# Two heads side by side in the 64-row halves of the matmul array, for the scores and their maxima in a fused attention kernel

## The chip, the cores and the metric

The kernel runs on one core of one Trainium2 chip. The metric is the device time of one launch in microseconds; the lower the better. Times given for a kernel are medians of several executions; what is read from a trace comes from one more, profiled, execution.

## What is computed

The input is 32 images of 128 channels by 32 x 32 positions, so 1024 tokens of 128 channels each. Every image goes through three layers:

```python
# layer 0: group norm, one-head attention over 1024 tokens (width 128), residual
h = group_norm(x)
q, k, v = split(qkv_w @ h + qkv_b)
x = x + proj(softmax(q.T @ k / sqrt(128)) @ v)
t = tokens(x)
# layer 1: eight search heads of width 16, two shared retrieval values
u = layer_norm(t)
sq, sk, rq = heads(u @ wq_s), heads(u @ wk_s), heads(u @ wq_r)      # 8 heads of 16
rv = u @ wv_r                                                        # 2 values of 16
retrieved = softmax(sq @ sk.T / 4) @ rv                              # per head and value
gate = softmax(sum(rq * (retrieved @ wk_ret)) / 4)                   # over the 2 values
t = t + (sum(gate * retrieved)) @ w_out
# layer 2: a block-quantised 128 x 128 weight and a second weight
t = t + (layer_norm(t) @ lora.T) @ W.T
```

The eight heads' score matrices of 1024 x 1024 are the bulk: each is made twice, once for the row maxima and once, transposed and with the maximum subtracted, for the exponentials.

## The kernel before

An image's layer 1 is worked in four **phases** (two groups of four heads by two halves of 512 queries) of eight **steps** (key tiles of 128), 32 steps in all. A software pipeline runs over the images: in one pass of the loop the scores and values of image b (`HEAD`), the last stages of image b-1 (`TAIL`) and the first ones of b+1 and b+2 (`FRONT`, `NEXT`) stand mixed. `schedule()` makes the list: for each step, which stages are issued and in which order, from a position between 0 and 1 that each gets. Every engine runs the same list in program order (`in_order`), takes what is its own, and waits on semaphores for the rest. Images 1 to 29 are a hardware loop (`engine.Fori`, L213), the first and last three are written out.

The stages that matter here:

- `scores` (L799 on TensorE, PE for short): one matmul for one head, key tile by 512 queries, into one PSUM bank; ScalarE (ACT) reads it with an exponential into `p1` (L982). Four a step.
- `max1` (L776): the same product the other way round (query tile by 512 keys) for the *next* phase; VectorE (DVE) takes the row maximum (L1072). 32 a phase, spread over the steps so that VectorE's load is even.
- `max_rows1` (L784): at the end of a phase the maxima, negated by VectorE (L1076), are transposed by TensorE, and ScalarE writes the rows into `q_stack` (L950). The next phase's scores wait for it.
- `values` (L810): rv times `p1` for four heads at once, four matmuls of 32 output columns side by side, two passes each (fp32). GpSimd (POOL) adds the same `p1` into `p_sum` (L627), seven adds a phase, and `den` (L819) sums that over the partitions once a phase, two steps into the next one. GpSimd's first add of a phase waits until `den` of the phase before has been read (L990).
- All of these share six PSUM banks (`ps_bank`), taken in turn. A matmul waits until the reader of its bank, six uses back, is done.

The operands are kept as a high and a low part. For a head, `q_stack` and `k_stack` hold three blocks of 32 rows (hi/hi, hi/lo, lo/hi) of which the head uses 16 in each block, and a fourth block of 32 rows for the maxima; `max1` reads 96 rows, `scores` 128. SyncE (SP) builds these stacks from SBUF to SBUF with 36 DMAs an image (L541, L546).

## Time and profile before

| | |
|---|---|
| median of 3 runs | 5834.74 us (5830.56 to 5835.21) |
| the profiled execution | 5838.83 us, its span 5836.5 us |
| TensorE matmul | 5436.7 us busy, 93% |
| GpSimd | 4251.2 us, 73% |
| VectorE | 3955.0 us, 68% |
| ScalarE | 3470.2 us, 59% |
| granted TensorE clock | 0.981 of full |

Busy time of TensorE counts a matmul from its start to its modelled end. Matmuls are pipelined, so the next may start before that; what one costs is the distance from its start to the start of the next, which the timeline shows.

### The profile page before, as it was taken

What the parts mean: (1) busy time and instruction counts of PE and PEld (TensorE: products, weight loads), DVE (VectorE), ACT (ScalarE), POOL (GpSimd) and SP (SyncE); (2) the same over time, 40 slices, a digit from 0 to 9 for tenths busy, and PEclk for the clock granted to TensorE, in tenths of its full rate; (3) what the DMA queues carried; (4) which work ended last, traced back from release to release, by engine and by line L of the source; (5) the groups of instructions that cost most, each with busy time, mean ns of one, the idle gap of its engine ahead of it and who ended that gap; (6) DMA issues with size and microseconds to landing.
All of it is one profiled execution on the core that took longest, in us unless ns stands there. A gap on an engine that the chain in (4) does not pass through costs nothing.

```text
span 5836.5 us, 99943 instructions
## 1 busy us (share of the span) xinstructions
PE 5436.7 (93%) x30350; PEld 3295.9 (56%) x30350; DVE 3955.0 (68%) x8189; ACT 3470.2 (59%) x6689; POOL 4251.2 (73%) x1109
## 2 busy tenths in 40 slices
PE   5999999999999999999999999999999999999986
PEld 3555555565555555555555555555555555556543
DVE  4776667667676666676667676677766676766763
ACT  2566566656566565666565665666665656665654
POOL 1677777777777777777777777777777777777787
PEclk9999999999999999999999999999999999999998
DMA  1101110111111111111111111111111111101110
GB/s 36 24 26 33 31 38 26 27 34 27 38 26 34 27 34 30 37 26 30 31 27 38 31 29 27 34 30 38 26 34 27 27 37 36 28 24 36 23 33 11
DMA packets 64867, 176.65 MB, mean 30 GB/s; under 512 B 21856, under 2 KB 23264, under 8 KB 64224
## 3 DMA queue, kind: packets, MB, share of 16 engines
q1 hardware_dynamic: 64224, 168.61, 12.3%
q8 instruction: 339, 5.55, 0.4%
q14 instruction: 304, 2.49, 0.1%
HBM read 17.53 MB, written 16.78 MB: 6 GB/s over the span
## 4 chain that ended last, share of the span: by engine, by line
PE 79%; DVE 9%; ACT 5%; issue 4%; POOL 2%; SPq 0%; DMA 0%; DVEq 0%; ACTq 0%; POOLq 0%
PE ps_bank L776 16%; PE ps_u L810 16%; PE ps_bank L799 15%; PE ps_bank L763 7%; PE ps_bank L691 4%; PE ps_bank L679 3%; DVE max_part L1062 3%; DVE max_part L1072 3%; PE ps_bank L747 2%; PE ps_bank L819 2%; PE ps_bank L750 2%; PE ps_bank L749 2%; PE ps_bank L748 2%; POOL p_sum L627 2%; ACT work L963 2%
## 5 line engine op out<-in xcount | busy, mean ns | idle before, releaser
L627 POOL TENSOR_TENSOR p_sum<-p_sum,p 128x2048 f32<-128x2048 f32 x768 | 3509.0, 4569 | 411.4 <-ACT p L982 381.2
L1072 DVE TENSOR_REDUCE max_part<-ps_bank 128x1 f32<-128x512 f32 x4096 | 2613.7, 683 | 1237.9 <-PE ps_bank L776 1224.9
L982 ACT ACTIVATE p<-ps_bank 128x512 f32<-128x512 f32 x4096 | 2283.6, 599 | 1495.3 <-PE ps_bank L799 1482.6
L799 PE MATMUL ps_bank<-q_stack,k_stack 128*128 128x512 f32 x4096 | 1726.3, 438 | 25.1 <-DVE t_front L1096 20.7
L776 PE MATMUL ps_bank<-k_stack,q_stack 96*128 96x512 f32 x4096 | 1594.6, 426 | 25.9 <-DVE max_part L1072 11.2
L776 PEld LDWEIGHTS ps_bank<-k_stack,q_stack 96*128 96x128 f32 x4096 | 777.6, 193 | 687.5 <-DVE max_part L1072 287.2
L627 POOL TENSOR_TENSOR p_sum<-p 128x2048 f32<-128x2048 f32 x128 | 584.3, 4565 | 792.4 <-ACT den_sb L990 731.3
L799 PEld LDWEIGHTS ps_bank<-q_stack,k_stack 128*128 128x128 f32 x4096 | 766.2, 192 | 655.1 <-issue 273.2
L810 PE MATMUL ps_u<-p,rv 128*32 128x512 f32 x8192 | 1114.5, 617 | 19.1 <-ACT u_sb L987 12.2
L763 PEld LDWEIGHTS ps_bank<-v,p 128*128 128x128 f32 x4096 | 494.1, 191 | 17.8 <-issue 2.4
L763 PE MATMUL ps_bank<-v,p 128*128 128x129 f32 x4096 | 498.2, 274 | 1.6 <-ACT p L939 1.6
L939 ACT ACTIVATE p<-ps_bank 128x512 f32<-128x512 f32 x512 | 306.3, 598 | 325.1 <-PE ps_bank L750 322.1
L1062 DVE TENSOR_REDUCE max_part<-ps_bank 128x1 f32<-128x512 f32 x512 | 316.9, 681 | 117.8 <-PE ps_bank L728 117.8
L810 PEld LDWEIGHTS ps_u<-p,rv 128*32 128x32 f32 x8192 | 162.5, 108 | 369.1 <-issue 298.2
L747 PE MATMUL ps_bank<-q_hi,k_hi 128*128 128x512 f32 x512 | 219.2, 428 | 112.4 <-issue 87.7
L605 POOL TENSOR_TENSOR rstd<-var,minus_half 128x8 f32<-128x8 f32 x64 | 105.6, 1650 | 273.7 <-DVE var L1109 273.7
L749 PE MATMUL ps_bank<-max_row,first_row 128*128 128x512 f32 x512 | 204.6, 400 | 0.0
L750 PE MATMUL ps_bank<-q_hi,k_lo 128*128 128x512 f32 x512 | 204.2, 399 | 0.0
L748 PE MATMUL ps_bank<-q_lo,k_hi 128*128 128x512 f32 x512 | 203.9, 398 | 0.0
L747 PEld LDWEIGHTS ps_bank<-q_hi,k_hi 128*128 128x128 f32 x512 | 97.7, 191 | 181.5 <-issue 152.1
L1095 DVE RECIPROCAL den<-ps_bank 128x1 f32<-128x1 f32 x256 | 41.9, 164 | 213.6 <-PE ps_bank L763 211.8
L728 PE MATMUL ps_bank<-k_hi,q_hi 128*128 128x512 f32 x512 | 167.3, 418 | 2.3 <-DVE k_lo L1054 1.6
(140 smaller groups left out, 4600.2 us busy)
## 6 DMA issues: line engine op xcount, KB each, us to landing
q_stack<-q_hi SPq DMA_DIRECT2D x256, 128.0 KB, 2.4
k_stack<-k_hi SPq DMA_DIRECT2D x512, 64.0 KB, 2.3
x_sb<-in_x SPq DMA_DIRECT2D x32, 512.0 KB, 3.3
t_held<-t_front SPq DMA_DIRECT2D x32, 512.0 KB, 2.9
k_stack<-k_lo SPq DMA_DIRECT2D x256, 64.0 KB, 2.4
q_stack<-q_lo SPq DMA_DIRECT2D x128, 128.0 KB, 2.3
t_core<-t_held SPq DMA_DIRECT2D x32, 512.0 KB, 3.4
out_y<-out_sb SPq DMA_DIRECT2D x32, 512.0 KB, 2.6
```

What stands on the lines that cost most here:

```text
L627: pool.tensor_tensor(p_sum[:, :, :], before, p1[:, step % ring, :, :], ALU.add)\
L747: pe.matmul(out, k_hi[0][:, keys], q_hi[0][:, queries], start=True, stop=False)
L748: pe.matmul(out, k_hi[0][:, keys], q_lo[0][:, queries], start=False, stop=False)
L749: pe.matmul(out, first_row[:, :], max_row0[:, queries], start=False, stop=False)
L750: pe.matmul(out, k_lo[0][:, keys], q_hi[0][:, queries], start=False, stop=True).then_inc(filled, 1)
L763: last = pe.matmul(out[:, 0:P + 1], p0[:, key_tile, at:at + P], v0[:, key_tile, :], start=(key_tile == 0), stop=(key_tile == tiles - 1))
L776: pe.matmul(out, q_stack[0:3 * QUAD, head // 2, at:at + P], k_stack[0:3 * QUAD, head, half * HALF:(half + 1) * HALF], start=True, stop=Tru ...
L799: pe.matmul(out, k_stack[:, head, keys], q_stack[:, head // 2, queries], start=True, stop=True)\
L810: last = pe.matmul(ps_u[n * QUAD:(n + 1) * QUAD, :], rv[:, key_tile, :], p1[:, step % ring, n, :], start=(key_tile == 0), stop=(key_tile = ...
L982: act.activation(p1[:, step % ring, n, :], read_bank(), ACT.Exp, scale=scale1)\
L1062: dve.tensor_reduce(max_part0[:, i, half:half + 1], read_bank(), AXIS.X, ALU.max)\
L1072: dve.tensor_reduce(max_part1[:, i, n, half:half + 1], read_bank(), AXIS.X, ALU.max)\
```

## The change

Five edits, made together.

1. The three products of a head are laid out with interleaved rows (`PARTS` = 4: rows 0, 4, 8, ... hold the first, 1, 5, 9, ... the second), so that a head needs 64 rows instead of 128. The heads of a pair lie in rows 0 to 63 and 64 to 127 of both stacks. `max1` and `scores` then take 63 and 64 rows, and each pair of matmuls stands next to each other in the list.
2. The stacks are built with 24 DMAs an image of 32 rows each. Rows 63 and 127 hold the maxima: ScalarE writes them to `max_row1`, and SyncE moves them with two DMAs a phase (`move_rows`); the next phase's scores wait for these.
3. No maxima stand in the last step of a phase: 32 uses are dealt, in twos, to the first seven steps. `max_rows1` stands at 0.05 of the last step instead of 0.85. All maxima stand right behind pairs of scores.
4. `values` of two steps are issued together in every second step, and `den` stands beside them. The transposes of the maxima turn 128 columns instead of 32.
5. The loops get `hint_back_edge=True`.

```diff
 for phase in range(4):
-        load[7] += LAST_STEP_LOAD
-        for _ in range(32):
-            least = min(range(8), key=lambda n: load[n] + count[n])
-            count[least] += 1
+        for _ in range(16):
+            least = min(range(7), key=lambda n: load[n] + count[n])
+            count[least] += 2
...
-            behind = ("HEAD", "values", step - 1) if step else ("TAIL", "values", 31)
-            placed.append((VALUES_AT if n else 0.02, behind))
-            placed += [(SCORES_AT + SCORES_SPREAD * m, ("HEAD", "scores", (step, m))) for m in range(4)]
-            end = 0.75 if n == 7 else 1.0
-            placed += [(end * (m + 0.5) / len(maxima), one) for m, one in enumerate(maxima)]
+            if step % 2 == 0:
+                for late in (2, 1):
+                    behind = ("HEAD", "values", step - late) if step else ("TAIL", "values", 32 - late)
+                    placed.append((VALUES_AT if n else 0.02, behind))
+            placed += [(VALUES_AT, one) for one in steps[step] if one[1] == "den"]
+            placed += [(SCORES_AT + SCORES_SPREAD * 2 * (m // 2), ("HEAD", "scores", (step, m))) for m in range(4)]
+            placed += [(SCORES_AT + SCORES_SPREAD * 2 * (m // 2), one) for m, one in enumerate(maxima)]
             if n == 7:
-                placed.append((0.85, (image, "max_rows1", ahead)))
+                placed.append((0.05, (image, "max_rows1", ahead)))
...
-    with engine.Fori(1, images - 2) as b:
+    with nc.Fori(1, images - 2, engines=[engine.engine], hint_back_edge=True) as b:
...
-                            sp.dma_start(q_stack[part * QUAD:(part + 1) * QUAD, pair, :].bitcast(F32),
-                                         q_part[1][pair * QUAD:(pair + 1) * QUAD, :].bitcast(F32))\
-                              .then_inc(stacked[group], 16)
-                            for n in range(2):
-                                at, row = pair * QUAD + n * HEAD_DIM, part * QUAD + n * HEAD_DIM
-                                sp.dma_start(k_stack[row:row + HEAD_DIM, 2 * pair + n, :].bitcast(F32),
-                                             k_part[1][at:at + HEAD_DIM, :].bitcast(F32))\
-                                  .then_inc(stacked[group], 16)
+                            sp.dma_start(q_stack[part:2 * ROWS:PARTS, pair, :].bitcast(F32),
+                                         q_part[1][source, :].bitcast(F32)).then_inc(stacked[group], 16)
+                            sp.dma_start(k_stack[part:2 * ROWS:PARTS, pair, :].bitcast(F32),
+                                         k_part[1][source, :].bitcast(F32)).then_inc(stacked[group], 16)
+                def move_rows(b, phase):
+                    group, half = divmod(phase, halves)
+                    sp.wait_ge(max_row_ready[1], phases * b + phase + 1)
+                    for pair in range(GROUP // 2):
+                        sp.dma_start(q_stack[ROWS - 1:2 * ROWS:ROWS, group * GROUP // 2 + pair,
+                                             half * HALF:(half + 1) * HALF].bitcast(F32),
+                                     max_row1[2 * pair:2 * pair + 2, :].bitcast(F32)).then_inc(rows_moved, 16)
...
-                    pe.matmul(out, q_stack[0:3 * QUAD, head // 2, at:at + P],
-                              k_stack[0:3 * QUAD, head, half * HALF:(half + 1) * HALF],
+                    rows = slice(side * ROWS, (side + 1) * ROWS - 1)
+                    pe.matmul(out, q_stack[rows, pair, at:at + P],
+                              k_stack[rows, pair, half * HALF:(half + 1) * HALF],
                               start=True, stop=True).then_inc(filled, 1)
...
-                        pe.wait_ge(max_row_ready[1], phases * b + phase + 1)
-                        awaited = (max_row_ready[1],)
+                        pe.wait_ge(rows_moved, row_incs * (phases * b + phase + 1))
-                    pe.matmul(out, k_stack[:, head, keys], q_stack[:, head // 2, queries], start=True, stop=True)\
+                    pair, side = divmod(GROUP * group + n, 2)
+                    rows = slice(side * ROWS, (side + 1) * ROWS)
+                    pe.matmul(out, k_stack[rows, pair, keys], q_stack[rows, pair, queries], start=True, stop=True)\
                       .then_inc(filled, 1)
```

How this moves instructions, on TensorE first. The place is the seventh step of the first phase, in the loop body. `ps_bank<-q_stack,k_stack` is a score, `ps_bank<-k_stack,q_stack` a maximum, `ps_u<-p,rv` the values of four heads. Before:

```order
L645 ISA
L799 MATMUL ps_bank<-q_stack,k_stack 128x512
L645 REGISTER_ALU
L776 MATMUL ps_bank<-k_stack,q_stack 128x512
L645 REGISTER_ALU
L799 MATMUL ps_bank<-q_stack,k_stack 128x512
L808 ISA
L810 MATMUL ps_u<-p,rv 32x512 x4
L645 REGISTER_ALU
L799 MATMUL ps_bank<-q_stack,k_stack 128x512
```

After:

```order
L677 ISA
L831 MATMUL ps_bank<-q_stack,k_stack 128x512
L677 REGISTER_ALU
L831 MATMUL ps_bank<-q_stack,k_stack 128x512
L677 REGISTER_ALU
L809 MATMUL ps_bank<-k_stack,q_stack 128x512
L677 REGISTER_ALU
L809 MATMUL ps_bank<-k_stack,q_stack 128x512
L842 MATMUL ps_u<-p,rv 32x512 x4
L840 ISA
L842 MATMUL ps_u<-p,rv 32x512 x4
L831 MATMUL ps_bank<-q_stack,k_stack 128x512 x2
```

Scores and maxima stood singly and in turn; now they come in twos of one kind, and two steps' values follow each other.

The second place is the last step of that phase on TensorE, where the maxima are turned. Before, they come behind the step's scores:

```order
L810 MATMUL ps_u<-p,rv 32x512 x4
L645 REGISTER_ALU
L799 MATMUL ps_bank<-q_stack,k_stack 128x512
L645 REGISTER_ALU
L799 MATMUL ps_bank<-q_stack,k_stack 128x512
L781 REGISTER_ALU
L645 REGISTER_ALU
L784 MATMUL ps_bank<-ident,max_cols 32x128 x4
```

After, they stand ahead of all four scores:

```order
L795 MATMUL ps_bank<-v,p 128x129 x8
L814 REGISTER_ALU
L677 REGISTER_ALU
L817 MATMUL ps_bank<-ident,max_cols 128x128 x4
L677 REGISTER_ALU
L831 MATMUL ps_bank<-q_stack,k_stack 128x512
```

The turning moved ahead of four scores that had stood before it.

The third is SyncE's queue in the loop, from the stack of one group to the next image's. After:

```order
L561 DMA q_stack<-max_row 2x512 x2
L567 DMA out_y<-out_sb 128x1024
L578 DMA t_core<-t_held 128x1024
L561 DMA q_stack<-max_row 2x512 x2
L573 DMA t_held<-t_front 128x1024
L551 DMA q_stack<-q_hi 32x1024
```

Before, the three big transfers stood there alone; the moves of the maxima are new between them.

## Rows read from the trace of the kernel before

**Rows 1.** The page: span, busy time by engine, and the chain that ended last

```profile
span 5836.5 us, 99943 instructions
PE 5436.7 (93%) x30350; PEld 3295.9 (56%) x30350; DVE 3955.0 (68%) x8189; ACT 3470.2 (59%) x6689; POOL 4251.2 (73%) x1109
PE 79%; DVE 9%; ACT 5%; issue 4%; POOL 2%; SPq 0%; DMA 0%; DVEq 0%; ACTq 0%; POOLq 0%
```

**Rows 2.** Busy time in windows: three passes of the loop, the mean last

```profile
3000.00:3177.50 177.50, 168.36 (x949) 101.99 (x948) 122.87 (x255) 108.32 (x209) 132.15 (x33) 0.99 0.13 31
sum 532.50, PE 505.14 PEld 306.61 DVE 368.72 ACT 324.22 POOL 395.87; mean PE 168.38 PEld 102.20 DVE 122.91 ACT 108.07 POOL 131.96
```

**Rows 3.** Groups of instructions: busy us, mean ns of one, idle before

```profile
L627 POOL TENSOR_TENSOR p_sum<-p_sum,p 128x2048 f32<-128x2048 f32 x768 | 3509.0, 4569 | 411.4 <-ACT p L982 381.2
L1072 DVE TENSOR_REDUCE max_part<-ps_bank 128x1 f32<-128x512 f32 x4096 | 2613.7, 683 | 1237.9 <-PE ps_bank L776 1224.9
L982 ACT ACTIVATE p<-ps_bank 128x512 f32<-128x512 f32 x4096 | 2283.6, 599 | 1495.3 <-PE ps_bank L799 1482.6
L799 PE MATMUL ps_bank<-q_stack,k_stack 128*128 128x512 f32 x4096 | 1726.3, 438 | 25.1 <-DVE t_front L1096 20.7
L776 PE MATMUL ps_bank<-k_stack,q_stack 96*128 96x512 f32 x4096 | 1594.6, 426 | 25.9 <-DVE max_part L1072 11.2
L810 PE MATMUL ps_u<-p,rv 128*32 128x512 f32 x8192 | 1114.5, 617 | 19.1 <-ACT u_sb L987 12.2
```

**Rows 4.** Timeline: start, duration, engine, instruction; matmuls in an unbroken row

```profile
3001.68 0.39 PE L747 MATMUL ps_bank<-q_hi,k_hi 128*128 128x512 f32 x1
3001.91 0.39 PE L748 MATMUL ps_bank<-q_lo,k_hi 128*128 128x512 f32 x1
3002.60 0.40 PE L776 MATMUL ps_bank<-k_stack,q_stack 96*128 96x512 f32 x1
3002.83 0.39 PE L799 MATMUL ps_bank<-q_stack,k_stack 128*128 128x512 f32 x1
```

**Rows 5.** Timeline: a visit of the values, and what stands around it

```profile
3005.16 0.40 PE L799 MATMUL ps_bank<-q_stack,k_stack 128*128 128x512 f32 x1
3005.49 1.06 PE L810 MATMUL ps_u<-p,rv 128*32 128x512 f32 x8
3006.49 0.50 PE L776 MATMUL ps_bank<-k_stack,q_stack 96*128 96x512 f32 x1
3006.83 0.40 PE L799 MATMUL ps_bank<-q_stack,k_stack 128*128 128x512 f32 x1
```

**Rows 6.** Timeline: TensorE across the loop's edge

```profile
2992.58 0.60 PE L784 MATMUL ps_bank<-ident,max_cols 128*32 128x128 f32 x4
2996.47 0.49 PE L747 MATMUL ps_bank<-q_hi,k_hi 128*128 128x512 f32 x1 [3.29 <-issue]
```

**Rows 7.** Timeline: readers with full banks before them

```profile
2955.77 2.07 ACT L982 ACTIVATE p<-ps_bank 128x512 f32<-128x512 f32 x4 [0.84 <-PE ps_bank L799]
...
3007.03 2.48 DVE L1072 TENSOR_REDUCE max_part<-ps_bank 128x1 f32<-128x512 f32 x4 [0.61 <-PE ps_bank L776]
```

**Rows 8.** Timeline: GpSimd's adds, and the way from its last add to the next phase

```profile
2942.59 13.87 POOL L627 TENSOR_TENSOR p_sum<-p_sum,p 128x2048 f32<-128x2048 f32 x3 [2.07 <-ACT p L982]
...
3008.10 1.06 PE L819 MATMUL ps_bank<-p_sum,ones 128*32 128x512 f32 x8
3009.24 0.59 ACT L990 COPY den_sb<-ps_bank 128x512 f32<-128x512 f32 x1 [0.89 <-PE ps_bank L819]
3009.90 4.55 POOL L627 TENSOR_TENSOR p_sum<-p 128x2048 f32<-128x2048 f32 x1 [11.54 <-ACT den_sb L990]
...
3038.98 1.65 POOL L605 TENSOR_TENSOR rstd<-var,minus_half 128x8 f32<-128x8 f32 x1 [4.65 <-DVE var L1109]
```

**Rows 9.** The maxima's copy, a DMA pair in SyncE's queue, and DMAs to landing

```profile
3041.95 1.00 ACT L950 CAST q_stack<-ps_bank 32x1024 fp32r<-32x1024 f32 x1
3005.51 1.23 SPq L546 DMA_DIRECT2D k_stack<-k_hi  x2
q_stack<-q_lo SPq DMA_DIRECT2D x128, 128.0 KB, 2.3
```

More of the change, by code:

```diff
@@ L22 @@
 QUAD = 32
+ROWS = 64
+PARTS = 4
 GROUPS_L0 = 8
@@ L43 @@
                "max_rows1": 0.45, "values": 0.95}
-VALUES_AT = 0.3
+VALUES_AT = 0.09
 SCORES_AT = 0.08
@@ L132, in schedule @@
             early = [other for other in steps[step] if other[1] in ("gate", "evict_u", "take_values")]
+            by_columns = [other for other in steps[step] if other[1] == "den"]
             placed = [(0.0, one) for one in early]
@@ L190, in wait, with in_order @@
         engine.wait_ge(sem, value)
-def in_order(engine, steps, images, stages, banks=None, links=None, first=None):
+def in_order(nc, engine, steps, images, stages, banks=None, links=None, first=None):
     def image_of(b, kinds):
@@ L372, in _ @@
                     sp.dma_start(qkv_bias[:, :], qkv_b.rearrange("(t o) -> o t", o=P)).then_inc(weights_loaded, 16)
+                sp.wait_ge(stacks_cleared, 1)
+                for pair in range(PAIRS):
+                    sp.dma_start(k_stack[ROWS - 1:2 * ROWS:ROWS, pair, :].bitcast(F32), out_sb[0:2, :])\
+                      .then_inc(ones_rows_ready, 16)
                 sp.wait_ge(blocks_zeroed, 1)
@@ L510, in all_images @@
             p1_ready = sem("p1_ready")
+            rows_moved = sem("rows_moved")
             p1_summed = sem("p1_summed")
@@ L628, in add_weights @@
                         .then_inc(p1_summed, 1)
-                in_order(pool, steps, images, {"values": add_weights, "norm_group_var": rstd0,
+                in_order(nc, pool, steps, images, {"values": add_weights, "norm_group_var": rstd0,
                                                "ln1_stats": rstd_shift(0), "ln2_stats": rstd_shift(1)})
@@ L783, in max_rows1 @@
                     for i in range(tiles_per_half):
-                        last = pe.transpose(out[0:QUAD, i * P:(i + 1) * P], max_cols1[:, i, :], ident[:, :])
+                        last = pe.transpose(out[:, i * P:(i + 1) * P], max_cols1[:, i, :], ident[:, :])
                     last.then_inc(filled, 1)
@@ L857, in tensor_program @@
                 }
-                in_order(pe, steps, images, stages, banks, first=first_of_image)
+                in_order(nc, pe, steps, images, stages, banks, first=first_of_image)
             def scalar_program(act):
@@ L946, in max_rows1 @@
                 def max_rows1(b, phase):
-                    group, half = divmod(phase, halves)
-                    pairs = slice(group * GROUP // 2, (group + 1) * GROUP // 2)
-                    act.copy(q_stack[3 * QUAD:, pairs, half * HALF:(half + 1) * HALF],
-                             read_bank()[0:QUAD, :].unsqueeze(1).broadcast_to([QUAD, GROUP // 2, HALF]))\
-                       .then_inc(max_row_ready[1], 1)
+                    wait(act, rows_moved, row_incs * (phases * b + phase))
+                    act.copy(max_row1[:, :], read_bank()[0:QUAD, :]).then_inc(max_row_ready[1], 1)
                 def rqk_part(half):
@@ L1017, in scalar_program @@
                 }
-                in_order(act, steps, images, stages, banks)
+                in_order(nc, act, steps, images, stages, banks)
             def vector_program(dve):
@@ L1070, in max1 @@
                     phase, use = arg
-                    i, n, half = use // (GROUP * halves), use // halves % GROUP, use % halves
+                    i, two, half, side = use // (GROUP * halves), use // (2 * halves) % 2, use // 2 % halves, use % 2
+                    n = 2 * two + side
                     dve.tensor_reduce(max_part1[:, i, n, half:half + 1], read_bank(), AXIS.X, ALU.max)\
@@ L1186, in vector_program @@
                 }
-                in_order(dve, steps, images, stages, banks, links)
+                in_order(nc, dve, steps, images, stages, banks, links)
             with nc.Block() as block:
```

54 lines of the change are left out of this document (35 added, 19 removed).

## The prediction, written before the result was known

> **What bounds the kernel now.** I read the page first. TensorE's matmuls are busy 93% of the span and make 79% of the chain that ended last; VectorE has 68%, ScalarE 59%, GpSimd 73% [rows 1]. One pass of the loop takes 177.5 us, and the windows of three passes repeat within 0.5 us: TensorE 168.4 busy, VectorE 122.9, ScalarE 108.1, GpSimd 132.0, at a clock of 0.99 [rows 2]. The groups say the same from the readers' side: VectorE's maxima and ScalarE's exponentials sat idle for 1238 and 1495 us, nearly all for the matmul that fills their bank, while the matmuls themselves waited under 30 us a group [rows 3]. So TensorE's order of work sets the pass.
>
> What a matmul costs is read as the distance of starts. In an unbroken row a 512-column matmul starts every 0.23 us (3002.60, 3002.83), though each lasts 0.40, and 96 or 128 rows make no difference [rows 4]. A pass has 128 scores and 128 maxima, 59.6 us at 0.233. A visit of the values is eight matmuls of 32 columns in which four run side by side, two times 0.43 us, and its neighbours pay for it: the matmul ahead of it holds 0.33 instead of 0.23, and the next one starts 1.00 after it [rows 5]. That is about 0.10 us for each change of the array's shape. Adding up the body of the loop this way (scores and maxima 59.6; 36 visits of values and `den` at 0.90, 32.4; layer 0's 64 score matmuls 15.0 and 128 value passes at 0.112, 14.4; projections and turns 30.4; 81 changes of shape 7.8) gives 159.6 us. The loop's edge adds 3.3 us in which TensorE waits for nothing that the profile shows [rows 6]. The other 14.6 us are waits for banks and for stages.
>
> **What the change does, part by part.**
>
> Pairs. If both halves work at once, 256 matmuls become 128 pairs. The trace has no two row halves at work. The nearest row is the values' visit, where four column strips run side by side in the time of one [rows 5]. From it I take a pair at 0.24 us: 30.7 for 59.6, **-28.9 us a pass**. The bounds are 0.24 and, if one runs after the other, 0.47, which gives nothing.
>
> The Trainium skill (TensorE: Matmul & The Clock Gate, Part 3) has tiles in distinct row groups start some 4 ns apart. By that the term would be the same 29 us; no run here shows it for rows yet.
>
> Changes of shape. Counted over the built order, the body goes from 81 to 101 changes between whole array, 32 columns and 64 rows: pairs are islands among whole-array work, which costs 46 entries, while doubled visits of the values and turns over 128 columns take changes away. At 0.10 each [rows 5], **+2.0 us**. Below, a change could be free (-8); above, the load of the weights is laid bare for both halves, some 0.2 an entry (+5 more).
>
> The Trainium skill (TensorEngine Tiling, Key Properties) says that changing the tiling mode drains TensorE, which speaks against this change. The trace agrees that a change costs, with 0.10 us; a full drain of a 0.40 us matmul each time would be 0.17, and 101 of them 17 us instead of 10.
>
> Loop hint. The edge costs TensorE 3.29 us [rows 6], in 29 passes. If the next code is there in time, **-3.3 us**; no row shows a hinted loop, so the bounds are 0 and -3.3. I take the whole, since nothing else is waited for there.
>
> Sum for TensorE: 177.5 - 28.9 + 2.0 - 3.3 = **147.3 us** with today's waits kept, and 132.6 with none.
>
> Readers. They lose nothing of their work, only the 1.00 us copy of maxima gets shorter [rows 9]. With full banks before it VectorE takes a maximum every 0.60 us ((2.48 - 0.68)/3) and ScalarE an exponential every 0.49 ((2.07 - 0.60)/3) [rows 7]. Pricing each of the 32 steps so for each engine, TensorE is the slowest in nearly all steps before. After, it isn't: steps with six maxima cost VectorE 3.6 us and more and TensorE 1.4 to 2.4. Six banks let TensorE run about one step ahead. The sum of the slowest engine by step is 166.2 before and 156.9 after; in windows of two steps 162 before and 145 to 149 after. Today's pass without its edge, 174.2, is 8 above the first and 12 above the second. The same distances after give 155 to 165.
>
> GpSimd. Three adds take 13.87, so one every 4.65, seven 32.5 us; from `den` on TensorE over ScalarE's copy to the next add it is 1.80 us (3008.10 to 3009.90) [rows 8]. Four phases are 137.2, and the 1.65 + 0.2 us for a layer norm and about 1 us for the group norm in its queue make **a floor of 140 us**. Today 11.5 us of idle before a phase's first add hide this [rows 8]; after, that is nearly gone. TensorE waits in order at `den`.
>
> The maxima's way. After the turn comes ScalarE's copy, then SyncE's two DMAs, two in 1.23 us to issue and 2.3 to land [rows 9]: 3.5 us that were not there. In the meantime TensorE has four scores, 0.9 to 2 us of layer 0 and two visits of values, of which the second waits for the last four exponentials anyway (2.0 us, [rows 7]). So I take 0, with 1 us for each of four phases at most. The turn itself now waits for VectorE's last maxima, one to three at 0.60: about 1 us a phase, **+4**. The stacks need 24 instead of 36 issues; SyncE's queue isn't waited for, so 0.
>
> I take a pass of **153 us**: between TensorE's 147.3 (+4 for the turns) and the 155 of the readers' two-step windows.
>
> The sum against the profiled execution, 5838.8 us: the stages save 177.5 - 3.3 - 153 = 21.2 us an image, 32 images (the six written out make up the three that the loop lacks) 678 us; the edge saves 29 x 3.3 = 96. That leaves 5065. The median of the runs is 4 us under the profiled one: **5060 us**, a ratio of 0.867.
>
> **The rivals.**
>
> *Banks and readers bind harder.* Pairs empty the six banks in 0.7 us while a bank comes back only after matmul, queue and reader, over 1.6 us. For it: the readers' sum by step. Against: half of the banks' time lies beside values and layer 0. A pass of 162 to 165: 5350 to 5440 us. Chance 0.17.
>
> The Trainium skill (TensorEngine Tiling, PSUM Bottleneck) says the same, that tiling speeds TensorE up but not the emptying of PSUM. By the trace the readers have 54 and 69 us of slack in a pass, which it thus bears out only in part [rows 2].
>
> *A pair is only half side by side*, because two loads of 128 columns follow each other, or the second bank is late: 0.34 a pair, the distance seen where a load isn't hidden [rows 5]. A pass of 147.3 + 12.8 = 160, 5290 us. Chance 0.10.
>
> *The halves run one after the other.* The change then does only the rest: 177.5 + 2.0 - 3.3 = 176.2, and 5839 + 64 - 96 = 5807, less 4: 5803, faster by 0.5%. Chance 0.03.
>
> *Slower.* The same, and each of the 46 entries into the half-array shape lays its loads bare. From 0.10 us an entry the gain of the hint is gone; at 0.23 it is 10.6 us a pass, 5803 + 340 = 6140 us. Against it speaks the values' visit [rows 5]. Chance 0.05.
>
> *As forecast*, 4800 to 5250: chance 0.65.
>
> **How the numbers follow.** The low end is a pass of 145 (GpSimd's floor and some waits), 32 x 29.2 + 96 off: 4800. The high end takes in half a pair side by side and most of the readers' case: a pass of 162, 5350. So 4800 to 5350. A measurement of this kernel tells 0.2% from no change. Faster 0.94, within it 0.01, slower 0.05.
>
> **What would show it.** Scores and maxima of a pair start within 0.01 us, pairs 0.23 to 0.25 apart in a row. TensorE's busy share falls under 90%, VectorE's rises to about 80%, GpSimd's to 86%. The idle time before GpSimd's first add falls from the 11.5 us shown [rows 8] to 2 or 3. The 3.29 us at the edge are gone. Wrong would be starts 0.23 apart within a pair; a wait for `rows_moved` of several us in each phase; a lower granted clock; or the edge as it was.

## The result

The changed kernel takes 6230.47 us (median of 4 runs, 6225.93 to 6245.47), the one before 5833.13 beside it: a ratio of 1.0686 [1.0667, 1.0705], slower by 6.9% where 13% faster was forecast. (Two of the four runs of `e5_short_after`, below, were over 1.5% above its fastest; its time is that of the other two.) The page of the changed kernel, in the parts that [rows 1] and [rows 3] show of before:

```profile
span 6230.8 us, 100137 instructions
PE 5716.2 (92%) x30350; PEld 2989.1 (48%) x30350; DVE 3930.5 (63%) x8182; ACT 3343.5 (54%) x6689; POOL 4233.0 (68%) x1109
PEclk8889888898889898888988899988889888989887
PE 74%; DVE 11%; ACT 8%; issue 5%; POOL 1%; SPq 0%; ACTq 0%; DMA 0%; DVEq 0%; POOLq 0%
L659 POOL TENSOR_TENSOR p_sum<-p 128x2048 f32<-128x2048 f32 x128 | 581.2, 4541 | 1362.7 <-ACT den_sb L1019 1303.5
L1102 DVE TENSOR_REDUCE max_part<-ps_bank 128x1 f32<-128x512 f32 x4096 | 2554.7, 682 | 1389.8 <-PE ps_bank L809 1378.1
L1011 ACT ACTIVATE p<-ps_bank 128x512 f32<-128x512 f32 x4096 | 2173.3, 602 | 1343.9 <-PE ps_bank L831 1328.6
L809 PE MATMUL ps_bank<-k_stack,q_stack 63*128 63x512 f32 x4096 | 1305.5, 489 | 70.4 <-ACT p L1011 35.1
L831 PE MATMUL ps_bank<-q_stack,k_stack 64*128 64x512 f32 x4096 | 1196.9, 510 | 108.6 <-DVE k_lo L1080 77.5
L842 PE MATMUL ps_u<-p,rv 128*32 128x512 f32 x8192 | 1200.7, 711 | 8.6 <-ACT p L1011 8.5
```

The busy time of scores and maxima did fall, from 3321 to 2502 us together. But TensorE stayed at 92%, all readers fell in share, the values' matmuls grew from 617 to 711 ns with the same work, and the granted clock went from 0.981 to 0.887. Scores now wait 77.5 us for `k_lo` on VectorE. They don't read it: in the code a score waits for the reader of its bank, six uses back, and in a phase's first step for the moved maxima. `k_lo` is such a reader, so this too is a wait for a bank. Before a phase's first add GpSimd waits 1304 us in all; before it was 731.

Windows of the changed kernel (length, then busy us and count of PE, PEld, DVE, ACT, POOL; clock; DMA share; GB/s): one pass of the loop, then three stretches around one long step.

```profile
2987.60:3178.70 191.10, 178.52 (x952) 93.40 (x948) 122.42 (x255) 104.42 (x209) 131.61 (x33) 0.88 0.10 28
3105.00:3112.00 7.00, 6.63 (x29) 2.91 (x21) 5.69 (x19) 4.51 (x9) 5.65 (x3) 0.82 0.19 75
3112.00:3120.00 8.00, 8.00 (x33) 2.65 (x34) 3.56 (x6) 1.62 (x6) 0.00 (x0) 0.52 0.01 2
3120.00:3128.00 8.00, 4.37 (x20) 2.96 (x18) 2.64 (x5) 6.32 (x15) 4.51 (x1) 0.69 0.00 0
```

A pass takes 191.1 us instead of 177.5. The timeline of those stretches, and two rows of a calmer place at the head:

```profile
3000.32 0.50 PE L831 MATMUL ps_bank<-q_stack,k_stack 64*128 64x512 f32 x2
3000.66 0.40 PE L809 MATMUL ps_bank<-k_stack,q_stack 63*128 63x512 f32 x2
...
3103.58 1.92 PE L842 MATMUL ps_u<-p,rv 128*32 128x512 f32 x16
...
3106.67 0.99 PE L809 MATMUL ps_bank<-k_stack,q_stack 63*128 63x512 f32 x2 [0.27 <-ACT p L1011]
...
3109.12 2.93 PE L809 MATMUL ps_bank<-k_stack,q_stack 63*128 63x512 f32 x6
3109.50 6.06 DVE L1102 TENSOR_REDUCE max_part<-ps_bank 128x1 f32<-128x512 f32 x10
...
3113.23 1.39 PE L809 MATMUL ps_bank<-k_stack,q_stack 63*128 63x512 f32 x2
3114.55 3.64 PE L842 MATMUL ps_u<-p,rv 128*32 128x512 f32 x16
3117.96 1.90 PE L851 MATMUL ps_bank<-p_sum,ones 128*32 128x512 f32 x8
3119.94 0.59 ACT L1019 COPY den_sb<-ps_bank 128x512 f32<-128x512 f32 x1 [5.46 <-PE ps_bank L851]
3120.56 2.48 DVE L1102 TENSOR_REDUCE max_part<-ps_bank 128x1 f32<-128x512 f32 x4 [5.00 <-PE ps_bank L809]
3120.60 4.51 POOL L659 TENSOR_TENSOR p_sum<-p 128x2048 f32<-128x2048 f32 x1 [9.01 <-ACT den_sb L1019]
3124.70 1.96 PE L747 MATMUL ps_bank<-ident,work 128*128 128x128 f32 x8 [3.63 <-ACT work L992]
3126.59 0.79 PE L831 MATMUL ps_bank<-q_stack,k_stack 64*128 64x512 f32 x2
```

The two matmuls of the pair at 3000.32 take 0.50 us together, so they do run side by side, and the next pair starts 0.34 behind. Not all do: over the whole trace 66% of the scores and maxima start within 0.02 us of another one. The rest start singly, as from 3106.67 on, where two maxima take 0.99 us. At 3109.12 six maxima take 2.93 us, one every 0.51: that is near VectorE's reads, ten in 6.06, and far from the 0.23 of a matmul alone [rows 4]. Then come 24 matmuls that fill one bank among them (the values go to `ps_u`). They take 5.2 us, since the clock is at 0.52 in that window, nearly all of it at the 1.2 GHz level; at 3103.58 the same sixteen values' matmuls took 1.92. Meanwhile ScalarE waits 5.46 us, VectorE 5.00, GpSimd 9.01. From the first score at 3112.50 to the next step's at 3126.59 are 14.1 us, and the step takes as much in every pass of the loop; before, from the same two scores' starts, it took 7.1. These 7 us are more than half of the 12.7 by which the pass grew (177.6 to 190.3, means over the loop). Part of them is TensorE's own wait of 3.63 us for ScalarE's `work`, which ScalarE, in its order, reaches only behind the copy of `den`; the same wait was 1.93 us in a pass of the kernel before.

### The profile page after: what moved, and what is told of

It reads as the page before. It is cut to its first block, busy times and chain, and to the rows that moved or that the text cites. A ratio compares the mean times of both kernels' runs of the same rounds, so it can differ in the third digit from the quotient of the medians.

```text
span 6230.8 us, 100137 instructions
## 1 busy us (share of the span) xinstructions
PE 5716.2 (92%) x30350; PEld 2989.1 (48%) x30350; DVE 3930.5 (63%) x8182; ACT 3343.5 (54%) x6689; POOL 4233.0 (68%) x1109
## 4 chain that ended last, share of the span: by engine, by line
PE 74%; DVE 11%; ACT 8%; issue 5%; POOL 1%; SPq 0%; ACTq 0%; DMA 0%; DVEq 0%; POOLq 0%
PE ps_u L842 18%; PE ps_bank L831 11%; PE ps_bank L809 10%; PE ps_bank L795 8%; DVE max_part L1102 5%; PE ps_bank L711 4%; ACT work L992 3%; PE ps_bank L723 3%; ACT p L1011 3%; PE ps_bank L779 2%; PE ps_bank L851 2%; DVE max_part L1091 2%; PE ps_bank L747 2%; PE ps_bank L760 2%; PE ps_bank L781 2%
## 5 line engine op out<-in xcount | busy, mean ns | idle before, releaser
L1011 ACT ACTIVATE p<-ps_bank 128x512 f32<-128x512 f32 x4096 | 2173.3, 602 | 1343.9 <-PE ps_bank L831 1328.6
L809 PE MATMUL ps_bank<-k_stack,q_stack 63*128 63x512 f32 x4096 | 1305.5, 489 | 70.4 <-ACT p L1011 35.1
L831 PE MATMUL ps_bank<-q_stack,k_stack 64*128 64x512 f32 x4096 | 1196.9, 510 | 108.6 <-DVE k_lo L1080 77.5
L842 PE MATMUL ps_u<-p,rv 128*32 128x512 f32 x8192 | 1200.7, 711 | 8.6 <-ACT p L1011 8.5
L831 PEld LDWEIGHTS ps_bank<-q_stack,k_stack 64*128 64x128 f32 x4096 | 486.0, 195 | 865.2 <-issue 474.3
L809 PEld LDWEIGHTS ps_bank<-k_stack,q_stack 63*128 63x128 f32 x4096 | 594.4, 204 | 516.8 <-ACT p L1011 282.0
L842 PEld LDWEIGHTS ps_u<-p,rv 128*32 128x32 f32 x8192 | 234.1, 122 | 624.2 <-issue 456.3
L971 ACT ACTIVATE p<-ps_bank 128x512 f32<-128x512 f32 x512 | 302.5, 597 | 298.3 <-PE ps_bank L782 297.6
L1019 ACT COPY den_sb<-ps_bank 128x512 f32<-128x512 f32 x128 | 75.1, 586 | 452.4 <-PE ps_bank L851 452.4
L747 PE MATMUL ps_bank<-ident,work 128*128 128x128 f32 x512 | 101.0, 360 | 165.9 <-ACT work L992 126.9
L1158 DVE TENSOR_TENSOR ps_tok<-ps_tok,den_inv 128x512 f32<-128x512 f32 x128 | 89.0, 695 | 146.0 <-PE ps_tok L866 146.0
```

What stands on the lines that cost most here:

```text
L809: pe.matmul(out, q_stack[rows, pair, at:at + P], k_stack[rows, pair, half * HALF:(half + 1) * HALF], start=True, stop=True).then_inc(fille ...
L831: pe.matmul(out, k_stack[rows, pair, keys], q_stack[rows, pair, queries], start=True, stop=True)\
L842: last = pe.matmul(ps_u[n * QUAD:(n + 1) * QUAD, :], rv[:, key_tile, :], p1[:, step % ring, n, :], start=(key_tile == 0), stop=(key_tile = ...
L971: act.activation(p0[:, n % tiles, :], read_bank(), ACT.Exp, scale=scale0).then_inc(p0_ready, 1)
L1011: act.activation(p1[:, step % ring, n, :], read_bank(), ACT.Exp, scale=scale1)\
```

## The experiments

Each was timed beside the kernel before; the numbers are the median, the ratio and the granted clock. The kernel before itself read 5831 to 5838 us beside them, so differences of some 10 us between experiments say nothing.

**The parts one by one: `e1_order`, `e2_rows`, `e3_hint`, and `e4_cross`.** The first has the kernel before's whole-array stacks and matmuls, and the change's order, turns over 128 columns and hint:

```diff
-            behind = ("HEAD", "values", step - 1) if step else ("TAIL", "values", 31)
-            placed.append((VALUES_AT if n else 0.02, behind))
+            if step % 2 == 0:
+                for late in (2, 1):
+                    behind = ("HEAD", "values", step - late) if step else ("TAIL", "values", 32 - late)
+                    placed.append((VALUES_AT if n else 0.02, behind))
+            placed += [(SCORES_AT + SCORES_SPREAD * 2 * (m // 2), ("HEAD", "scores", (step, m))) for m in range(4)]
+            placed += [(SCORES_AT + SCORES_SPREAD * 2 * (m // 2), one) for m, one in enumerate(maxima)]
...
-                    i, n, half = use // (GROUP * halves), use // halves % GROUP, use % halves
+                    i, two, half, side = use // (GROUP * halves), use // (2 * halves) % 2, use // 2 % halves, use % 2
+                    n = 2 * two + side
```

> The kernel before with the changed kernel's order of work, its turns over 128 columns and the loop hint, but with the stacks, the whole-array matmuls and ScalarE's direct write of the maxima as they were. Theory A (the half-array shape itself draws the granted clock down, which was 0.887 in the changed kernel against 0.981): the clock comes back to about 0.98, and the time is near that before, 5750 to 5900 us. Theory B (the order in clusters starves the readers and TensorE waits for banks; the clock falls because TensorE stands still): the clock stays at about 0.90 and the time is 6200 us or more, since nothing runs side by side.

6028.98 us, 1.0342, clock 0.968: the clock came back for the most part, the time only by 201 of 397 us, and neither theory's range was met. The second has the change's stacks and half arrays, with the list of the kernel before:

```diff
-            placed += [(SCORES_AT + SCORES_SPREAD * 2 * (m // 2), ("HEAD", "scores", (step, m))) for m in range(4)]
-            placed += [(SCORES_AT + SCORES_SPREAD * 2 * (m // 2), one) for m, one in enumerate(maxima)]
+            placed += [(SCORES_AT + SCORES_SPREAD * m, ("HEAD", "scores", (step, m))) for m in range(4)]
+            end = 0.75 if n == 7 else 1.0
+            placed += [(end * (m + 0.5) / len(maxima), one) for m, one in enumerate(maxima)]
...
-                placed.append((0.05, (image, "max_rows1", ahead)))
+                placed.append((0.85, (image, "max_rows1", ahead)))
```

> The changed kernel with the order of work of the kernel before (scores and maxima in turn, values each step, maxima in the last step too, the turn at 0.85), with the half-array matmuls, the new stacks, the moves of the maxima and the hint kept. Theory A: the clock stays low, 0.90 or less, and the time is 6200 us or more. Theory B: the clock is 0.95 or more and the time 5600 to 5850 us. If the maxima's move over SyncE is what costs, TensorE waits several us at the first score of each phase here, more than in the changed kernel, since the turn stands later.

5917.79 us, 1.0151, clock 0.966, 68 us above theory B's range. This list stands partly against half arrays: 59% of the scores and maxima start beside another one, and a pass has 93 changes between half and whole array, against 69 in the changed kernel. Its maxima turn late in the last step, and the DMA shows there, as it hardly does in the changed kernel (30.1 us in 35 waits):

```profile
PE ps_bank L830 <- DMA q_stack<-max_row: 93.8, 98, 1.9
```

The third is the kernel before with the hint alone:

```diff
-    with engine.Fori(1, images - 2) as b:
+    with nc.Fori(1, images - 2, engines=[engine.engine], hint_back_edge=True) as b:
```

> The kernel before with the loop hint alone. Both theories: 29 passes lose 3.3 us each at the edge, so 5740 us (ratio 0.984); if the hint does nothing, 5835 us.

5737.66 us, 0.9842: 93 us less than beside it, where 29 x 3.3 = 96 were taken. In the timeline at the edge nothing is left of the 3.29 us of [rows 6]:

```profile
2982.69 0.60 PE L784 MATMUL ps_bank<-ident,max_cols 128*32 128x128 f32 x4
2983.05 0.48 PE L747 MATMUL ps_bank<-q_hi,k_hi 128*128 128x512 f32 x1
```

The fourth is the changed kernel with pairs of one score and one maximum, so that a pair's two banks go to two readers:

```diff
-            placed += [(SCORES_AT + SCORES_SPREAD * 2 * (m // 2), ("HEAD", "scores", (step, m))) for m in range(4)]
-            placed += [(SCORES_AT + SCORES_SPREAD * 2 * (m // 2), one) for m, one in enumerate(maxima)]
+            placed += [(SCORES_AT + SCORES_SPREAD * 2 * (m // 2) + 0.001 * (m % 2), ("HEAD", "scores", (step, m)))
+                       for m in range(4)]
+            placed += [(SCORES_AT + SCORES_SPREAD * 2 * (m // 2) + 0.001 * (m % 2) + 0.0005, one)
+                       for m, one in enumerate(maxima)]
...
-                    i, two, half, side = use // (GROUP * halves), use // (2 * halves) % 2, use // 2 % halves, use % 2
+                    i, two, half, side = use // (GROUP * halves), use // (2 * halves) % 2, use // 2 % halves, 1 - use % 2
```

> The changed kernel with each pair made of one score and one maximum (heads chosen so that they lie in different halves), in place of two scores and then two maxima: both readers get a bank at once. Theory A (clock by shape): no change in the clock, time within 1% of 6230 us. Theory B (readers are fed in bursts of two for one of them): fewer waits, 6000 us or less, clock 0.90 or more.

6145.96 us, 1.0541, clock 0.898: 85 us better, no more, where theory B wanted 6000 or less. So against the hinted kernel (5738) the order alone costs 291, the half arrays alone 180, both 493; and mixed pairs don't heal it. No single part is the culprit.

**Do readers set the pace? `e5_short_after` and `e6_short_before`.** ScalarE's exponentials and VectorE's maxima read 256 of a bank's 512 columns (half of the keys are left out of the maxima, and half of each `p1` tile is a constant), in the changed kernel and in the hinted one:

```diff
+                dve.memset(p1[:, :, :, :], 0.5)
-                    act.activation(p1[:, step % ring, n, :], read_bank(), ACT.Exp, scale=scale1)\
+                    act.activation(p1[:, step % ring, n, 0:HALF // 2], read_bank()[:, 0:HALF // 2], ACT.Exp, scale=scale1)\
-                    dve.tensor_reduce(max_part1[:, i, n, half:half + 1], read_bank(), AXIS.X, ALU.max)\
+                    dve.tensor_reduce(max_part1[:, i, n, half:half + 1], read_bank()[:, 0:HALF // 2], AXIS.X, ALU.max)\
```

> The changed kernel, but ScalarE's exponentials and VectorE's maxima of layer 1 read only the first 256 of a bank's 512 columns (the other halves of p1 hold a constant; half of the keys are left out of the maxima). TensorE's work is the same; a bank comes back about 0.25 us sooner, and both readers do half. If six banks and their readers are what eats the gain of the pairs, TensorE's own work now shows: 5100 to 5500 us, well under the kernel before with the same cut. If it is the shape of the array (clock, changes of shape), it stays near 6000 us with the clock at 0.89.

> The kernel before with the loop hint, and the same cut of both readers to 256 columns. It is bound by TensorE, so little comes of it: 5500 to 5650 us, against 5738 with full reads. If banks bound it as well, 5400 or less.

5550 us (5518 and 5582; ratio 0.951 [0.945, 0.957]) and 5572.89 us (0.9548 [0.9534, 0.9561]), clocks of the profiled executions 0.951 and 0.991. The same cut takes about 680 us off the changed kernel and 165 off the hinted one. Banks and their readers bind the changed kernel about four times as hard. But the two are not told apart by these times, where the first was expected at 5500 or less and well under the second: something else holds it too.

**Which part of the order? `e7_single`, `e8_turn_late`, `e9_whole_single`, `e10_double_before`.** `e7_single` is the changed kernel with the values once a step, behind more of the step's scores; `e9_whole_single` is `e1_order` with the same edit; `e10_double_before` is `e3_hint` with double visits, the reverse of the lines above the dots (its visits stay at 0.3):

```diff
-            if step % 2 == 0:
-                for late in (2, 1):
-                    behind = ("HEAD", "values", step - late) if step else ("TAIL", "values", 32 - late)
-                    placed.append((VALUES_AT if n else 0.02, behind))
+            behind = ("HEAD", "values", step - 1) if step else ("TAIL", "values", 31)
+            placed.append((VALUES_AT if n else 0.02, behind))
...
-VALUES_AT = 0.09
+VALUES_AT = 0.3
```

> The changed kernel with the values visited once in every step again, at 0.3. Two visits in a row leave both readers without a new bank for 1.9 us; single ones for 1.0. If these gaps are what the order costs, 6050 us or less and a clock of 0.91 or more, in spite of some 15 changes of shape more a pass (1.5 us a pass, 50 us in all); if not, 6250 to 6300 us.

> The kernel of the order alone on whole-array matmuls (6029 us), with the values visited once a step as in the run of single visits (5741 us, which has the half-array pairs). The two differ only in the shape of the array, the stacks and the way of the maxima, so this prices the pairs under the better order. If the pairs gain nothing because six banks and two readers set the rate of scores and maxima, it comes within 1.5% of 5741. If the pairs do gain their 29 us a pass, it is slower by 300 us or more: 6040.

> The kernel before with the hint (5738 us) and the values of two steps visited together in every second step, nothing else. Theory: a visit of 1.9 us without a bank leaves both readers dry, and the steps without values are set by the readers; so 5850 to 6000 us. If double visits cost only together with clusters of maxima and half arrays, 5700 to 5760 us (some 80 us less for 16 changes of shape fewer on either side, given back in part).

5740.89 us (0.9836, clock 0.964), 5842.49 (1.0016 [1.0006, 1.0026], 0.982) and 5749.24 (0.9856, 0.986). Double visits at 0.09 instead of single ones at 0.3 cost 490 us on half arrays and 187 on the whole array in the same order; in the old order, double visits at 0.3 cost 12, which is not clear of noise, and not the 110 or more that the theory wanted. So they harm in the new order and more so with half arrays. That the clusters of maxima are what makes the difference between the orders is likely but not shown: the place of the visit, of `den` and of the turn differ too, and no run parts the doubling from its place.

The traces show where the 490 us lie. In passes of the loop, 13.4 of the 16.2 us between the changed kernel and `e7_single` are longer distances from one score or maximum to the next. `e9_whole_single` lies 1.8% above `e7_single`, between the two cases expected. `e8_turn_late` moves the turn of the maxima back:

```diff
-                placed.append((0.05, (image, "max_rows1", ahead)))
+                placed.append((0.85, (image, "max_rows1", ahead)))
```

> The changed kernel with the maxima turned at 0.85 of a phase's last step, as before, in place of 0.05 (still no maxima in that step). If TensorE's wait for VectorE's last maxima costs, it gains; but ScalarE's copy and SyncE's DMAs then have less time before the next phase's scores. I expect the wait for the moved rows to grow by 1 to 2 us a phase: 6300 to 6450 us.

6255.23 us, 1.0712 [1.0694, 1.0729], which is not clear of the changed kernel's 1.0686 [1.0667, 1.0705] and less than expected. In the changed kernel the waits for the moved rows are 30.1 us in all, about 1 us a pass.

**The clock: `e11_twice`.** The changed kernel, each maximum's matmul issued twice into its bank. TensorE gets 4096 matmuls more; banks, readers and order stay:

```diff
-                    pe.matmul(out, q_stack[rows, pair, at:at + P],
-                              k_stack[rows, pair, half * HALF:(half + 1) * HALF],
-                              start=True, stop=True).then_inc(filled, 1)
+                    for again in range(2):
+                        last = pe.matmul(out, q_stack[rows, pair, at:at + P],
+                                         k_stack[rows, pair, half * HALF:(half + 1) * HALF],
+                                         start=True, stop=True)
+                    last.then_inc(filled, 1)
```

> The changed kernel with every matmul for a maximum issued twice into the same bank. It adds TensorE work of 15 to 30 us a pass (500 to 900 us in all) just where TensorE stands waiting for a bank. If the fall of the granted clock, which follows such standing, is a main part of the loss, the clock rises to 0.93 or more and the time stays at 6250 us or falls. If the clock's fall comes from the half-array shape, or costs nothing since TensorE waits anyway, the time rises by 300 us or more.

6206.55 us (6175.24 to 6222.10), 1.0636 [1.0597, 1.0675], clock 0.956. More work, no more time. Its timeline at the visit that took 3.64 us above, and three passes (565.8 us), beside three of the changed kernel (573.3):

```profile
3100.45 3.03 PE L844 MATMUL ps_u<-p,rv 128*32 128x512 f32 x16
...
3116.23 1.92 PE L844 MATMUL ps_u<-p,rv 128*32 128x512 f32 x16
```

```profile
3000.00:3565.80 565.80, 536.48 (x3247) 303.25 (x3240) 368.15 (x767) 315.11 (x630) 398.25 (x100) 0.97 0.11 30
```

```profile
3000.00:3573.30 573.30, 536.40 (x2842) 279.86 (x2840) 365.64 (x763) 312.53 (x626) 394.76 (x100) 0.88 0.10 28
```

The mean clock is back at 0.97, though the clock still dips in places (3.03 us for the visit). Since the time doesn't grow by the 15 to 30 us a pass of added work, nearly all of it must lie in time in which TensorE waited for banks; it was not followed matmul by matmul.

**What pairs are worth when nothing else is wrong: `e12_cross_single`, `e13_short_cross`, `e14_short_whole`.** `e12_cross_single` has the edits of `e4_cross` and `e7_single` together; `e13_short_cross` and `e14_short_whole` are `e12_cross_single` and `e9_whole_single` with the short reads (and leave the same part out).

> The changed kernel with single visits of the values and with pairs of one score and one maximum. Single visits gave 490 us, mixed pairs 85; if both work on the same shortage of banks, 5680 to 5740 us, a little below the kernel of single visits (5741). If the two sum, 5650.

> The kernel of mixed pairs and single visits (5654 us), with both readers of layer 1 cut to 256 of 512 columns, as in the earlier runs with short reads (the other halves of p1 hold a constant, half of the keys are left out of the maxima). If the readers and their six banks eat the pairs' 29 us a pass, halving them frees it: 5000 to 5250 us. If what holds it is the chain of stages and TensorE's own changes of shape, which stay, 5450 to 5550 us.

> The same cut on the kernel with the new order, single visits and whole-array matmuls (5842 us). Its difference from the run of short reads with half-array pairs is the pairs' worth once readers are cheap. By the readers' theory: 5600 to 5650 here, 400 us or more above that run; otherwise 150 us or less above it.

5653.62 us (0.9695 [0.9679, 0.9711], clock 0.975), 5316.47 (0.9103) and 5586.13 (0.9567). `e12_cross_single` beats both kernels. The two gains, 490 and 85, add up to its 577, which by its expectation speaks against one shortage that both relieve. `e13_short_cross` lies between its two ranges, `e14_short_whole` just under its first, and the 270 us between them are neither the 400 nor the 150 expected. The page of `e12_cross_single`, its span and shares, then three passes of it:

```profile
span 5649.4 us, 100456 instructions
PE 5128.0 (91%) x30350; PEld 2709.1 (48%) x30350; DVE 3917.5 (69%) x8182; ACT 3392.6 (60%) x6689; POOL 4237.2 (75%) x1109
```

```profile
3000.00:3514.20 514.20, 477.16 (x2843) 252.16 (x2842) 364.65 (x764) 317.10 (x627) 395.38 (x99) 0.98 0.11 32
```

Half arrays against the whole array are worth 102 us with like pairs in one order (`e9_whole_single` to `e7_single`), 189 with mixed ones, and 270 with mixed ones and short reads. In the last two the order of scores and maxima within a group changes too; no run has the mixed order on the whole array. The forecast's term was 32 x 28.9 = 925: even with half the reading, 655 us of it are missing.

The traces of `e14_short_whole` and `e13_short_cross` show most of the missing part, at a full clock and with cheap readers. Two maxima between whole-array matmuls of layer 0, first on the whole array, then as a pair:

```profile
3032.00 0.39 PE L750 MATMUL ps_bank<-q_hi,k_lo 128*128 128x512 f32 x1
3032.23 0.63 PE L777 MATMUL ps_bank<-k_stack,q_stack 96*128 96x512 f32 x2
3032.69 0.40 PE L747 MATMUL ps_bank<-q_hi,k_hi 128*128 128x512 f32 x1
3032.93 0.40 PE L748 MATMUL ps_bank<-q_lo,k_hi 128*128 128x512 f32 x1
```

```profile
3055.35 0.40 PE L783 MATMUL ps_bank<-q_hi,k_lo 128*128 128x512 f32 x1
3055.67 0.51 PE L810 MATMUL ps_bank<-k_stack,q_stack 63*128 63x512 f32 x2
3056.11 0.50 PE L780 MATMUL ps_bank<-q_hi,k_hi 128*128 128x512 f32 x1
3056.44 0.40 PE L781 MATMUL ps_bank<-q_lo,k_hi 128*128 128x512 f32 x1
```

From the first start to the last are 0.93 us with the whole array and 1.09 with the pair. A pair alone among whole-array matmuls, an island of one pair, is slower here than two whole-array matmuls: it saves 0.23 and pays about 0.4 for going to half arrays and back. The median distance from a score or maximum to a whole-array matmul goes from 0.23 to 0.40 us, and the other way round from 0.03 to 0.20 (most of the matmuls ahead of it have 128 columns); the second whole-array matmul is held 0.1 longer too.

Worked out in the same way for all passes of the loop (the time from each matmul's start to the next one's, us a pass; half arrays less whole array):

| | `e9_whole_single` to `e7_single` | `e14_short_whole` to `e13_short_cross` | `e1_order` to the changed kernel |
|---|---|---|---|
| from score or maximum to the next | -23.4 | -27.2 | -17.4 |
| at the 69 or 70 changes between half and whole array | +10.1 | +10.9 | +11.3 |
| the first whole-array matmul behind scores or maxima, to the next | +3.0 | +3.2 | +3.3 |
| values and `den` | +1.9 | +0.7 | +7.1 |
| other matmuls | +1.0 | +0.7 | +1.0 |
| TensorE idle | +3.9 | +2.7 | +1.6 |
| the pass | -3.4 | -9.0 | +6.8 |

**Banks: `e15_4banks_hint` and `e16_4banks_cross`.** `e3_hint` and `e12_cross_single` with four banks.

```diff
-BANKS = 6
+BANKS = 4
```

> The kernel before with the hint (5738 us), with four PSUM banks taken in turn instead of six. A bank is then wanted back after four uses, 0.93 us of whole-array matmuls in a row, while the nearest reader needs 0.4 to 0.6 us to start and 0.6 to read. I expect TensorE to wait often: 6100 to 6500 us.

> The kernel of mixed pairs and single visits (5654 us) with four banks. Four uses are then two pairs, 0.47 us. If banks are what limits the pairs, it loses more than the whole-array kernel does, 700 us or more, and ends behind it; if not, both lose alike.

6197.71 us (1.0613) and 6629.67 (1.1355): 460 and 976 us lost. With half arrays two banks are worth twice as much. In the waits of the second (engine, what it waited for: us, times, longest), TensorE's weight loads for a score stand behind ScalarE's read:

```profile
PEld ps_bank L831 <- ACT p L1011: 475.2, 706, 1.9
```

With six banks the same wait is 244.3 us in 347 times. Both met their expectations.

## Why the prediction was wrong

**Steps that held.** Pairs run side by side where both banks are free, so the rival in which the halves follow each other is out. The one in which a pair is only half side by side because "the second bank is late" holds in part: 66% of scores and maxima start beside another one here, 78% in `e12_cross_single`, 89% in `e13_short_cross`. The hint gave its 3.3 us a pass. The maxima's way over SyncE stayed hidden but for about 1 us a pass. GpSimd's floor was never reached, so it bound nothing (the sum has one layer norm where the trace has two a pass, and should be 142).

**First failed step: "Pairs, -28.9 us a pass", taken off the path nearly in full, with "Changes of shape ... +2.0".** By `e9_whole_single` and `e7_single` the half arrays give 102 us over 32 images, 3.2 us a pass; with mixed pairs and short reads 8.4. By the table above, with cheap readers the pairs do save 27.2 of the 28.9, so that term was nearly right for TensorE alone. What was mis-sized is the change of shape. The prediction took 0.10 us from the values' visit for every kind of change; between half and whole array it measures 0.16 us in the mean, and 0.1 more behind each return to the whole array, 13 to 15 us a pass in all for the 69 or 70 of them. The prediction had worked out 0.17 for a matmul that must end first, and set it aside. Its rival *Slower* had the size, 10.6 us a pass, though for halves that don't overlap (and 46 entries at 0.10 would be 147 us, so the hint's 96 are gone from 0.065 on).

Most of the rest is banks and readers. With full reads the pairs save 23.4 instead of 27.2, and in the changed kernel 17.4: TensorE fills its banks in bursts and is then let on at the readers' rate, 0.51 us a maximum at 3109.12. I had read the trace of before as if there were nearly no such waits, since the matmuls' rows show under 30 us a group [rows 3]. A matmul lasts 0.40 us and the next can start after 0.23, so up to 0.17 us of waiting leaves TensorE busy, and the waits stand before the weight loads, as in this one of several rows of the kernel before:

```profile
PEld ps_bank L776 <- DVE max_part L1072: 287.2, 457, 1.6
```

In its rows of scores and maxima the starts lie about 336 us further apart in all than at 0.233 each. The rival of banks and readers names a part of the cause, but was priced with the same wrong reach: 5350 to 5440. With single visits it is 5741.

The Trainium skill (TensorEngine Tiling, PSUM Bottleneck) says that tiling speeds up TensorE but not the emptying of PSUM; `e16_4banks_cross` (976 us lost) and the short reads (about 680 us gained) bear it out here, more than I gave it.

**Second failed step: "Six banks let TensorE run about one step ahead", which made two-step windows of the readers' sum a fair bound.** The double visits, which I counted only as fewer changes of shape, put all bankless work of two steps into one place. In the steps without them TensorE is held at the readers' rate; when it comes to the sixteen values' matmuls and `den`, the banks run dry and both readers stand idle, 5.46 and 5.00 us at 3119.94. Six banks hold three uses for each reader, 3 x 0.60 = 1.8 us of VectorE's work, not a step's 3.6. GpSimd's idle time, forecast to shrink, rose to 1304 us, since `den` came late; the 11.5 us that the prediction took for it [rows 8] were the longest of a pass's four, the mean was 5.8 before and is 10.3 now. This is most of the 490 us between the changed kernel and `e7_single`, with the longer stretches at the low clock in it. The prediction's sums by step (166.2, 156.9) can't be followed row by row, so which of their steps were too low stays open but for the one above, 14.1 us.

**Third failed step: the sum was made at today's clock of 0.99.** The clock fell to 0.88 over a pass. A lower clock was named as a sign of being wrong, but had no term in the sum. Around the fall:

```profile
3106.00:3109.60 3.60, 3.23 (x13) 1.34 (x9) 3.29 (x15) 3.58 (x8) 2.81 (x1) 0.98 0.20 79
3109.60:3112.50 2.90, 2.90 (x9) 1.56 (x8) 2.90 (x6) 0.94 (x2) 1.85 (x2) 0.50 0.00 0
```

What TensorE did before it fell were bank-bound half-array matmuls, most of them single, 0.31 us apart in the mean from 3106.67 to 3109.12, with one idle time of 0.27 us. If a pass is split between the two levels, 0.88 means 24% of 191.1 us, 46, at 1.2 GHz, against 2% of 177.5, 4, before. At most half of these 46 are lost, 23 us a pass; where TensorE waits for a bank anyway, nothing is. In the visit it was 1.72 us of 3.64, with both readers dry. Clock and order can't be priced apart cleanly here: `e11_twice` gives most of the clock back, but fills the time with work, and the pass is 2.5 us shorter. So the clock made a dry stretch longer, and I can't say how long it would be by itself.

The Trainium skill (TensorE: Matmul & The Clock Gate, A second HAM failure mode) describes a kernel whose TensorE idles briefly and often on its PSUM banks, and whose clock swings between its levels for it. The trace agrees as to the swing, with 0.98 and then 0.50 in the windows above; before the fall the row at 3106.67 has the one idle time on a bank, 0.27 us.

**How the whole adds up.** From the hinted kernel's 5738: the new order without double visits costs 105 on the whole array (`e9_whole_single`), half arrays give 102 back, double visits, and their place, cost 490 on them; that is the 6230. The terms hold for this sequence of edits only: on the whole array the same double visits cost 187. Left open: why the new order costs 105 (1.9 of its 3.5 us a pass lie in the step that takes 14.1 us in the changed kernel: 9.7 against 7.7), how much of the 490 is the doubling and how much its place, and whether 63 and 64 rows by themselves lower the clock beyond making TensorE's work shorter.

## What to carry to other kernels

Count the places where half-array work meets whole-array work before splitting the array. Here an island of half-array matmuls cost about 0.4 us and a pair saved 0.23, so an island of one pair lost; islands want to be long, and no run here tried to join them. An engine that is busy 93% and in nearly all the chain may still wait for banks: look at the waits before its weight loads and at the distances of starts, and cut the reads or the banks as a test (460 or 976 us for two banks) before rewriting operands. With few banks and engines that run in order, spread the work that needs no bank between the work that does, and try giving neighbouring banks to different readers: `e12_cross_single` gained 577 us on the changed kernel by these two edits alone. Read the granted clock in windows beside a busy share: a high share can be slow matmuls.

## What the runs showed of the hardware

Going from half-array matmuls of 512 columns to whole-array ones, or back, cost 0.17 us in the median each way (0.23 to 0.40, and 0.03 to 0.20, `e14_short_whole` to `e13_short_cross`). Two matmuls in the two 64-row halves started mostly 3 to 4 ns apart where they started together.

TensorE's clock can fall to its 1.2 GHz level while its busy share is over 90%: in 3105 to 3112 it was busy 6.63 of 7.00 us at 0.82, and in the next 8.00 of 8.00 at 0.52. And giving it 13% more matmuls (34446 for 30350) raised the clock from 0.887 to 0.956 with no loss of time.
